# Attention kernel of two blocks: softmax sums of the first attention from a column of ones, and another split of the block copies

## The reference, cut to what matters

```python
# H = 16 heads, D = 16, L = 512 tokens, 16 batches
q = _layernorm(q, gq, bq)
k = _layernorm(k, gk, bk)
scores = jnp.einsum('nhld,nhmd->nhlm', q, k) * SM_SCALE
scores = jnp.where(causal, scores, NEG)
attn = jax.nn.softmax(scores, axis=-1)
out = jnp.einsum('nhlm,nhmd->nhld', attn, v)
out = out.transpose(0, 2, 1, 3).reshape(N, L, EMB)
return out @ Wo.T + bo
```

## Time and profile before

| what | value |
|---|---|
| median of three runs | 3756.36 us (3754.61 to 3757.57) |
| the profiled execution's own time | 3750.06 us |
| its span in the trace | 3748.4 us |
| mean granted clock of TensorE | 0.978 |
| busy, share of the span | PE 89%, PEld 71%, DVE 74%, ACT 64%, POOL 29% |

### The profile page before, as it was taken

One profiled execution on the slowest core, in us unless ns is written; L12 is line 12 of the kernel. 1 busy time (PEld: TensorE's weight loads), 2 busy tenths in 40 slices (PEclk: granted clock), 3 DMA queues, 4 the chain that ended last, 5 costly groups with the idle time before them and its releaser, 6 DMA issues.

```text
span 3748.4 us, 82331 instructions
## 1 busy us (share of the span) xinstructions
PE 3349.3 (89%) x31520; PEld 2643.7 (71%) x31584; DVE 2764.5 (74%) x5934; ACT 2408.6 (64%) x6426; POOL 1081.5 (29%) x762
## 2 busy tenths in 40 slices
PE   2599899998989999899998989989899998989988
PEld 2467677776767767677776767767677776767766
DVE  3676777777777777777777777777777777777775
ACT  1666667666666756667566666766667566676764
POOL 0424232232412324222242412424222242312420
PEclk9799999999999999999999999999999999999999
DMA  3000000000000000000000000000000000000000
GB/s 79 1 7 1 13 1 7 7 7 7 1 13 2 7 7 1 13 2 7 7 7 7 1 13 2 7 7 1 13 2 7 7 7 7 1 13 2 7 1 7
DMA packets 33765, 28.93 MB, mean 8 GB/s; under 512 B 8864, under 2 KB 33312, under 8 KB 33376
## 3 DMA queue, kind: packets, MB, share of 16 engines
q1 hardware_dynamic: 33376, 23.68, 2.2%
HBM read 15.28 MB, written 8.39 MB: 6 GB/s over the span
## 4 chain that ended last, share of the span: by engine, by line
PE 71%; ACT 13%; DVE 10%; issue 3%; POOL 2%; SPq 1%; DMA 0%; ACTq 0%; POOLq 0%; DVEq 0%
PE bank L664 14%; PE scores L773 11%; PE bank L675 8%; ACT prob L939 6%; PE scores L651 5%; PE bank L797 5%; PE scores L652 4%; PE scores L727 4%; PE scores L747 3%; PE bank L611 3%; PE scores L653 2%; PE bank L635 2%; DVE negmax L1176 2%; ACT qkt L885 2%; PE scores L647 1%
## 5 line engine op out<-in xcount | busy, mean ns | idle before, releaser
L939 ACT ACTIVATE prob<-scores,negmax 128x128 f32<-128x128 f32 (+3 forms) x2048 | 1059.2, 536 | 186.0 <-DVE negmax L1176 180.3
L1176 DVE TENSOR_REDUCE negmax<-scores 128x1 f32<-128x128 f32 (+3 forms) x2048 | 874.2, 484 | 56.8 <-PE scores L653 42.4
L664 PE MATMUL bank<-ident,prob 128*128 128x128 f32 x5120 | 725.8, 279 | 50.6 <-DVE probt L1184 43.6
L1184 DVE COPY probt<-bank 128x512 f32<-128x512 f32 x896 | 597.7, 685 | 170.4 <-PE bank L664 164.9
L664 PEld LDWEIGHTS bank<-ident,prob 128*128 128x128 f32 x5120 | 544.1, 141 | 163.8 <-issue 66.6
L653 PE MATMUL scores<-mask,ident 128*128 128x128 bf16 x2048 | 437.9, 225 | 0.0
L939 ACT ACTIVATION_READ_ACCUMULATOR prob<-scores,negmax 128x1 f32 x2048 | 435.0, 212 | 0.0
L651 PE MATMUL scores<-khh,qt 128*128 128x256 f32 (+2 forms) x1024 | 416.1, 407 | 13.2 <-POOL kll L544 13.2
L486 POOL TENSOR_TENSOR otl<-onm,oth 128x512 fp32r<-128x512 f32 x96 | 122.8, 1279 | 889.4 <-ACT oth L885 889.4
L497 POOL TENSOR_TENSOR rq<-ssq,expo 128x32 f32<-128x32 f32 x64 | 359.9, 5632 | 39.6 <-DVE ssq L1147 39.6
L481 POOL COPY rexp<-rsum 128x512 f32<-128x512 f32 x128 | 78.1, 610 | 981.4 <-DVE rsum L1188 981.4
(11 more groups left out here) (184 smaller groups left out, 6621.4 us busy)
## 6 DMA issues: line engine op xcount, KB each, us to landing
x_in<-in_x_rows SPq DMA_DIRECT2D x16, 512.0 KB, 3.7
out_rows<-x SPq DMA_DIRECT2D x16, 512.0 KB, 2.9
r_gu<-in_wg SPq DMA_DIRECT2D x2, 512.0 KB, 4.8
r_gu<-in_wu SPq DMA_DIRECT2D x2, 512.0 KB, 5.5
r_d<-in_wd SPq DMA_DIRECT2D x1, 1024.0 KB, 6.9
r_wqt<-in_wq_nope_t SPq DMA_DIRECT2D x1, 512.0 KB, 6.4
r_wqr<-in_wq SPq DMA_DIRECT2D x2, 256.0 KB, 8.2
r_wob<-in_wo SPq DMA_DIRECT2D x1, 512.0 KB, 5.1
```

Of the source, the lines that this page charges most:

```text
L664: ins = nc.tensor.transpose(bank[4 + n % 2][:, q * P:(q + 1) * P], prob[:, u % 2, q, i * P:(i + 1) * P], ident[:, :])
L939: nc.scalar.activation(prob[:, u % 2, q, 0:n], bank[q][:, 0:n], ACT.Exp, bias=negmax[:, a, u, q:q + 1], accum_out=sums[:, a, u, q:q + 1]). ...
L1176: nc.vector.tensor_reduce(negmax[:, a, u, M * part:M * part + M], scores[:, M * part:M * part + M, 0:n], axis=AX.X, op=ALU.max, negate=Tru ...
L1184: nc.vector.tensor_copy(probt[:, u % 2, i], bank[4 + n % 2][:, :]).then_inc(probt_dve.sem, 1)
```

## The change

In the first attention, for groups 0 to 2 (`COUNTED` = 3), the row sums no longer come from the exponentials. Column 16 of each head's values in `va` is set to one, so that the value product leaves the sum in row 16 of that head's 32 rows. When the group has been copied to `osb`, PE transposes `osb` into bank 7 (`transpose_counted`), and DVE takes the reciprocal of the sum columns straight from there (`invert_counted`). From then on all is as before: POOL spreads, PE transposes, DVE multiplies. The exponentials of those groups have no `accum_out`. Group 3 keeps its sums from the exponentials.

The steps move: `transpose_counted` to u % 4 == 1, `transpose_sums` and the reciprocal to u % 4 == 2, `normalise_out` to u % 4 == 3, and `split_out` to the end of ACT's iteration with u % 4 == 0, the next after that (u = 8, 12 and 16 for groups 0, 1 and 2).

The copies of the first attention are split anew: ACT has blocks 1, 3, 5, 7 and 9, DVE 0, 2, 4, 6 and 8. The second attention keeps its split and its order.

```diff
@@ -51,20 +51,21 @@
 BLOCKS = NG * NT * (NT + 1) // 2
 
 
-ACT_COPIES = tuple(n in (2, 5, 8) for n in range(NT * (NT + 1) // 2))
-
-
-def acts(n):
-    return ACT_COPIES[n % len(ACT_COPIES)]
-
-
-def act_count(n):
-
-    return sum(acts(i) for i in range(n))
-
-
-ACT_BLOCKS = act_count(BLOCKS)
-DVE_BLOCKS = BLOCKS - ACT_BLOCKS
+ACT_COPIES = ((1, 3, 5, 7, 9), (2, 5, 8))
+
+
+def acts(a, n):
+    return n % (NT * (NT + 1) // 2) in ACT_COPIES[a]
+
+
+def act_count(a, n):
+
+    return sum(acts(a, i) for i in range(n))
+
+
+ACT_BLOCKS = (act_count(0, BLOCKS), act_count(1, BLOCKS))
+DVE_BLOCKS = (BLOCKS - ACT_BLOCKS[0], BLOCKS - ACT_BLOCKS[1])
+COUNTED = NG - 1
 
@@ -304,8 +305,9 @@
     negmax_ready = Signal(sem("negmax_ready"), 2 * NM * UNITS)
     prob_ready = Signal(sem("prob_ready"), 2 * G * UNITS)
     probt_psum = Signal(sem("probt_psum"), 2 * BLOCKS)
-    probt_act = Signal(sem("probt_act"), 2 * ACT_BLOCKS)
-    probt_dve = Signal(sem("probt_dve"), 2 * DVE_BLOCKS)
+    probt_act = Signal(sem("probt_act"), sum(ACT_BLOCKS))
+    probt_dve = Signal(sem("probt_dve"), sum(DVE_BLOCKS))
+    osbt_psum = Signal(sem("osbt_psum"), COUNTED)
     pv_done = Signal(sem("pv_done"), 2 * UNITS)
     rsum_ready = Signal(sem("rsum_ready"), 2 * NG)
     rexp_ready = Signal(sem("rexp_ready"), 2 * NG)
@@ -370,9 +372,9 @@
 
     def block_copied(b, a, n):
 
-        if acts(n):
-            return probt_act.sem, probt_act.at(b, a * ACT_BLOCKS + act_count(n + 1))
-        return probt_dve.sem, probt_dve.at(b, a * DVE_BLOCKS + n + 1 - act_count(n + 1))
+        if acts(a, n):
+            return probt_act.sem, probt_act.at(b, a * ACT_BLOCKS[0] + act_count(a, n + 1))
+        return probt_dve.sem, probt_dve.at(b, a * DVE_BLOCKS[0] + n + 1 - act_count(a, n + 1))
 
     XT = (xth, xtl)
     EARLY = (1, 0, 1, 2)
@@ -463,6 +465,7 @@
         pool.wait_ge(weights_ready, len(SPLIT))
         nc.gpsimd.memset(va[:, :, :, :], 0.0).then_inc(va_zeroed, 1)
         pool.wait_ge(va_zeroed, 1)
+        nc.gpsimd.memset(va[:, :, :, D:D + 1], 1.0).then_inc(padded, 1)
         nc.gpsimd.memset(combt[:, :], 0.0).then_inc(padded, 1)
         for s in range(2):
             nc.gpsimd.memset(stk[:, s, :, SPLITS:SLOTS], 0.0).then_inc(padded, 1)
@@ -573,7 +576,7 @@
         last.then_inc(folded_psum, 1)
         pe.wait_ge(weights_ready, len(SPLIT))
         pe.wait_ge(va_zeroed, 1)
-        pe.wait_ge(padded, 3)
+        pe.wait_ge(padded, 4)
 
         def transpose_tokens(b, stage):
             for t in range(NT):
@@ -683,6 +686,14 @@
             for j in range(NT):
                 ins = nc.tensor.transpose(bank[7][:, ORDER[j] * P:(ORDER[j] + 1) * P], rexp[:, j].rearrange("p q r -> p (q r)"), ident[:, :])
             ins.then_inc(rsumt_psum.sem, 1)
+
+        def transpose_counted(b, g):
+            pe.wait_ge(osb_ready.sem, osb_ready.at(b, g + 1))
+            if g > 0:
+                pe.wait_ge(onm_ready.sem, onm_ready.at(b, g))
+            for j in range(NT):
+                ins = nc.tensor.transpose(bank[7][:, j * P:(j + 1) * P], osb[:, j * P:(j + 1) * P], ident[:, :])
+            ins.then_inc(osbt_psum.sem, 1)
 
         def attend(b, a, last):
             if a == 0 and b == 0:
@@ -704,7 +715,11 @@
                 transpose_prob(b, a, u, range(early))
                 if u > 0:
                     weigh_values(b, a, u - 1)
-                    if u % NT == 0:
+                    if a == 1 and u % NT == 0:
+                        transpose_sums(b, a, u // NT - 1)
+                    if a == 0 and u > NT and u % NT == 1:
+                        transpose_counted(b, u // NT - 1)
+                    if a == 0 and u > NT and u % NT == 2:
                         transpose_sums(b, a, u // NT - 1)
                 transpose_prob(b, a, u, range(early, tile_of(u) + 1))
             transpose_sums(b, a, NG - 1)
@@ -936,8 +951,12 @@
             if u >= 2:
                 act.wait_ge(probt_psum.sem, probt_psum.at(b, a * BLOCKS + first_block(u - 1)))
             for q in range(M * part, M * part + M):
-                nc.scalar.activation(prob[:, u % 2, q, 0:n], bank[q][:, 0:n], ACT.Exp, bias=negmax[:, a, u, q:q + 1],
-                                     accum_out=sums[:, a, u, q:q + 1]).then_inc(prob_ready.sem, 1)
+                if a == 0 and u < COUNTED * NT:
+                    nc.scalar.activation(prob[:, u % 2, q, 0:n], bank[q][:, 0:n], ACT.Exp,
+                                         bias=negmax[:, a, u, q:q + 1]).then_inc(prob_ready.sem, 1)
+                else:
+                    nc.scalar.activation(prob[:, u % 2, q, 0:n], bank[q][:, 0:n], ACT.Exp, bias=negmax[:, a, u, q:q + 1],
+                                         accum_out=sums[:, a, u, q:q + 1]).then_inc(prob_ready.sem, 1)
 
         def copy_block(b, a, u, i):
             n = first_block(u) + i
@@ -966,14 +985,16 @@
                 if u % NT == 1 and u > NT:
                     copy_out(b, a, u // NT - 1)
                 if 0 < u <= UNITS:
-                    mine = [i for i in range(tile_of(u - 1) + 1) if acts(first_block(u - 1) + i)]
+                    mine = [i for i in range(tile_of(u - 1) + 1) if acts(a, first_block(u - 1) + i)]
                 if u < UNITS and here:
                     for part in range(NM // 2, NM):
                         exps(b, a, u, part)
                 for i in mine:
                     copy_block(b, a, u - 1, i)
-                if u % NT == 2 and u > NT:
+                if a == 1 and u % NT == 2 and u > NT:
                     split_out(b, a, u // NT - 1)
+                if a == 0 and u % NT == 0 and u > NT:
+                    split_out(b, a, u // NT - 2)
             copy_out(b, a, NG - 1)
             split_out(b, a, NG - 1)
 
@@ -1054,7 +1075,7 @@
                 for part in range(NM):
                     exps(b + 1, 0, 0, part)
 
-        act.wait_ge(padded, 3)
+        act.wait_ge(padded, 4)
         split_first(0)
         for t in range(NT):
             copy_raw(0, t)
@@ -1187,6 +1208,11 @@
             dve.wait_ge(prob_ready.sem, prob_ready.at(b, (a * UNITS + (g + 1) * NT) * G))
             nc.vector.reciprocal(rsum[:, a, g * NT:(g + 1) * NT], sums[:, a, g * NT:(g + 1) * NT]).then_inc(rsum_ready.sem, 1)
 
+        def invert_counted(b, g):
+            dve.wait_ge(osbt_psum.sem, osbt_psum.at(b, g + 1))
+            counted = bank[7].rearrange("p (j q r) -> p j q r", j=NT, q=G)[:, :, :, D]
+            nc.vector.reciprocal(rsum[:, 0, g * NT:(g + 1) * NT], counted).then_inc(rsum_ready.sem, 1)
+
         def normalise_out(b, a, g):
             dve.wait_ge(rsumt_psum.sem, rsumt_psum.at(b, a * NG + g + 1))
             dve.wait_ge(osb_ready.sem, osb_ready.at(b, a * NG + g + 1))
@@ -1201,12 +1227,16 @@
                         maxima(b, a, u, part)
                 mine = []
                 if u > 0:
-                    mine = [i for i in range(tile_of(u - 1) + 1) if not acts(first_block(u - 1) + i)]
-                if u > 0 and u % NT == 0:
+                    mine = [i for i in range(tile_of(u - 1) + 1) if not acts(a, first_block(u - 1) + i)]
+                if u > 0 and u % NT == 0 and (a == 1 or u == UNITS):
                     invert_sums(b, a, u // NT - 1)
                 for i in mine:
                     copy_block(b, a, u - 1, i)
-                if u % NT == 1 and u > NT:
+                if a == 1 and u % NT == 1 and u > NT:
+                    normalise_out(b, a, u // NT - 1)
+                if a == 0 and u % NT == 2 and u > NT:
+                    invert_counted(b, u // NT - 1)
+                if a == 0 and u % NT == 3 and u > NT:
                     normalise_out(b, a, u // NT - 1)
 
             if a == 1 and not last:
```

## The result

The changed kernel takes 3910.79 us (median of four runs, 3907.69 to 3913.06) against 3756.34 before: ratio 1.0411, 95% interval 1.0393 to 1.0429. It is slower by 154 us, 9.65 us for each of the 16 batches. The clock did fall. One execution in all that follows, of e4_counted, fell in a slower state of the chip (4577 us) and is left out of its median.

A forecast was written before the change was run, and what follows sets the result against it. A ring of waits, with no engine full, was taken to bound the first attention's groups. Terms summed to 7.3 us a batch, times 16 = 117, on 3750.06 gives 3867, plus 6.3 for the median: 3873 us; range 3810 to 3928.

The forecast's parts named there:

- group 0: First head group of the first attention, without a counted part before it: 0.5 us lost per batch at block 3.
- groups 1 and 2: Middle head groups of the first attention: 14.13 us each instead of 13.16, so 0.97 lost per group, twice a batch.
- group 3 up to unit 15: Last head group: maxima about 0.62 us late, then exponentials with their sums pace ACT; 0.87 lost per batch.
- tail until PE goes on: End of the first attention: late split delays POOL's last copy, PE idles 3.3 us; 3.97 us lost per batch.
- clock: Rival, chance 0.20: PE's clock falls once more per batch behind the tail's idle, about 3.3 us a batch, 3926 us.
- The ring of waits: In each head group: maxima of unit 15, copy of block 3, block 5, next group; 13.16 us before the change.
- Block 3 behind the exponentials: Its copy, moved to ACT, waits for unit 15's last exponential: 0.55 us lost in every group.
- The later maxima: DVE's maxima of unit 15 start at 10.06 instead of 9.64 after the group's first score: 0.42 us lost.
- The term of the exponentials without accumulator reads: Two exponentials between the copy-out and unit 14's fourth score: 0.25 us saved together, ends 0 and 0.4.
- The forecast's own case: Whole kernel with all terms and no further clock fall: 3873 us, spanning 3845 to 3900, chance 0.58.
- The copy behind the exponential costs nothing: Rival, chance 0.14: groups stay at 13.16 us and only the first attention's tail is lost, 64 us, 3820.
- DVE's load is the bound: Rival, chance 0.05: groups shrink by DVE's saving, 4.5 us against 3.97 in the tail; 8 us gained, 3748.

The follow-up runs named there:

- e4_counted: Changed kernel with the first attention's copies split as in the kernel before (ACT 2, 5, 8), keeping the counted sums: 3804.5 us against 3754.3.
- e6: Changed kernel with DVE and ACT exchanging blocks 3 and 4 only (ACT 1, 4, 5, 7, 9): 3856.7 us, ratio 1.0275.
- e1: Changed kernel with POOL spreading group 3's reciprocals before its subtraction of group 2: 3829.3 us against 3754.3 for the kernel before.
- e2: Kernel before, with only ACT's split of group 2 in the first attention moved behind its copies of unit 15: 3806.4 us against 3754.3.
- e5: Changed kernel with 28 unused identity transposes on PE during its wait for the first attention's last reciprocals: 3877.6 us against 3753.8 for the kernel before.
- e9: Kernel before with the late split of group 2 and one small POOL operation more ahead of its last copy: 3829.8 us against 3753.8.
- e3: Kernel before with only the change's split of block copies (ACT 1, 3, 5, 7, 9), sums still from the exponentials: 3873.9 us against 3754.3.
- e7: Changed kernel with blocks 1 and 3 copied by DVE, 2 and 4 by ACT (ACT 2, 4, 5, 7, 9): 3829.0 us, ratio 1.0198.
- e10: e8 with the four transposes of the outputs moved on PE between the second and third score of unit 14: 3743.2 us against 3753.4 for the kernel before.
- e8: Changed kernel with ACT copying 2, 5, 8 and POOL's last reciprocals ahead of its subtraction of group 2: 3748.2 us against 3753.8 for the kernel before.

## Why the prediction was right or wrong, point by point

The first attention of the seventh batch, before and after, in the prediction's own terms (us per batch; from the lines above and the same lines of the two traces):

| term | predicted | measured |
|---|---|---|
| group 0 | 0.5 | 0.56 |
| groups 1 and 2 | 1.94 | 2.11 |
| group 3 up to unit 15 | 0.87 | 0.83 |
| tail until PE goes on | 3.97 | 3.79 |
| clock | 0 (rival: 3.3) | 2.60 |
| sum | 7.3 | 9.9 |

- **Groups 1 and 2.** They took 14.09 us each, 14.13 predicted. The measured loss is larger than the predicted one because the prediction took 13.16 as the old length of both, and group 2 took 12.91 before.
- **The bound: right.** The ring of waits decided, not the load. DVE lost 72 us of work and the kernel 154 us of time.
- **Block 3 behind the exponentials: right in place and size**, 0.55 predicted, 0.61 by e6 against the changed kernel. The page's busy shares spoke against it; the timeline of one group told it.
- **The later maxima: right.** They start 10.03 after the group's first score (1568.30, 0.39 behind the first line), 10.06 predicted; moving block 1 back to DVE gained 0.43 of the 0.42 forecast. The term of the exponentials without accumulator reads was a little large: the copy-out to the fourth score shrank by 0.18 and not 0.25.
- **The tail: right, and the largest term**, link by link: PE went on 6.49 after unit 15's transposes started, 6.67 predicted; most of the difference is POOL's copy, 1.21 behind its subtraction where 1.35 was taken. e1 took the fault out, e2 put it in alone.
- **The clock: the failed step.** The sum went by a clock that stays up, and the case in which it falls got a chance of 0.20. The argument against it was that 3.3 us (3.10 by the matmuls, as measured) are a little less than 3.45 and that shorter waits leave the clock up. But those shorter waits were all under 1 us; nothing in rows 3 and 4 lies near 3, so they said nothing on 3.3. Nearest to it was the one row that showed a fall, and the estimate should have gone by that. With the clock's case ahead the forecast would have been 3926, 15 too high, because its price was too large as well: 2.6 in the seventh batch, 2.07 on average by e5, not 3.3. The seventh batch is one of six in which the clock is low for 6.8 us in the tail; in the other ten it is 3.4. The Trainium skill, page "TensorE: Matmul & The Clock Gate", section "Why this matters for your kernels", warns of such gaps; the trace of the changed kernel and e9 agree with it, at 3.10 and 3.18 us of idle. In e3 the clock fell without such a gap.
- **The range.** The time lies in it only because the range was drawn out to the clock's case. The forecast's own case spanned 3845 to 3900 and missed, while e5, with the clock kept up, came to 3878.
- **The rivals.** "The copy behind the exponential costs nothing" fell with e6 and e3; "DVE's load is the bound" with e7: DVE has as few blocks there as in the changed kernel, and the groups ran near the old pace (13.31 against 13.16), not faster.

## What to carry to other kernels

When copies are shared between two engines, look at who waits for each one and at what stands ahead of it in its new queue; the count per engine comes second. When a step is put off, follow what it feeds through every in-order queue to the end of the stage, since the last round has no next unit to hide it. And when PE waits regularly, look at the granted clock behind the wait: in the kernel before, 28 matmuls without a use in the gap were worth 29.5 us, more than the counted sums (22.8).

## What the runs showed of the hardware

- Counted over all 16 batches of each trace, PE's granted clock fell in the tail of the first attention in 63 of 64 cases behind 3.10 to 3.19 us of idle matmuls (changed kernel, e6, e7, e9), in 3 of 32 behind 2.66 us (the first two batches of e2, the first of e4), and in all 16 of e3, where no wait of the attention is longer than 1.80 us. So one idle stretch's length told much here, but not all.
- The same 3.10 us of idle were followed by 3.4 us at the low clock in ten batches of the changed kernel and by 6.8 in six.
- A shorter stage ahead of a gap need not shorten the batch: e10's groups were together 1.3 us shorter than e8's, the low clock behind the gap lasted 10.2 instead of 6.8 us in ten batches, and these took the same 225 us. With the gap filled with 28 transposes the gain arrived.
- The accumulator read cost little: in the changed kernel exponentials of 256 columns start 0.45 us apart with it (1601.03 and 1601.48); without it two of 0.47 us take 0.84 together, so they start 0.37 apart. The reciprocal of 16 strided columns of PSUM took 0.25 us, as from SBUF.
